# Decoder layer on one core: x and its projections ahead of the context's K sums

## The reference

```
# 1. state space part, on layernorm(x)
xp = x @ x_proj_w.T                      # 16 + 2*16 = 48 columns: dt_in, B, C
dt = softplus(dt_in @ dt_proj_w.T + dt_proj_b)
h  = exp(dt * A) * h + dt * B * x        # scan over 128 tokens, 16 states x 512 channels
y  = sum_n(h * C) + D * x;    x = x + y
# 2. cross attention, 32 heads of 128, K and V from ctx (8 x 128 x 512)
k = ctx @ w_k.T;  v = ctx @ w_v.T        # each 1024 x 4096
x = x + (hidden + attention(rmsnorm(layernorm(x)), k, v, mask, bias))
# 3. linear with low rank experts, on layernorm(x);   x = x + out
```

## Time and profile before

| | |
|---|---|
| median of three runs | 993.68 us |
| profiled execution, its time | 994.63 us |
| its span in the trace | 992.5 us |
| PE busy | 938.2 us, 95% |
| DVE busy | 645.1 us, 65% |
| ACT busy | 486.3 us, 49% |
| POOL busy | 474.4 us, 48% |
| chain that ended last | PE 61%, DVE 27%, DMA 4%, ACT 3%, issue 3%, POOL 1% |

### The profile page before, as it was taken

The page is one execution under the profiler, slowest core; times in us unless marked ns, Lnnn a source line. Parts: engine busy times, 40 slices in busy tenths (PEclk is TensorE's granted clock), DMA queues, the critical chain, the costliest instruction groups (busy, mean ns, idle before and its releaser), DMA issues.

```text
span 992.5 us, 14723 instructions
## 1 busy us (share of the span) xinstructions
PE 938.2 (95%) x4648; PEld 772.2 (78%) x4648; DVE 645.1 (65%) x819; ACT 486.3 (49%) x1058; POOL 474.4 (48%) x291
## 2 busy tenths in 40 slices
PE   8996899989898989988999999999999999999998
PEld 7665677767686767766888888888888888888867
DVE  5289889999999999752454454544545444444675
ACT  4485354546354545243455545454454554545631
POOL 2112566666666666403445444554445544455422
PEclk9977999999899999999999999999999999999999
DMA  8345655655455543215744454444444444444302
GB/s 287 112 132 159 219 169 177 196 177 180 159 185 195 170 162 133 106 47 159 265 140 142 141 149 152 135 148 137 158 143 135 144 139 151 149 135 148 104 19 85
DMA packets 92315, 149.95 MB, mean 151 GB/s; under 512 B 10192, under 2 KB 34896, under 8 KB 92160
## 3 DMA queue, kind: packets, MB, share of 16 engines
q1 hardware_dynamic: 87888, 132.72, 41.7%
q10 hardware_dynamic: 4400, 16.91, 5.5%
HBM read 113.81 MB, written 35.78 MB: 151 GB/s over the span
## 4 chain that ended last, share of the span: by engine, by line
PE 61%; DVE 27%; DMA 4%; ACT 3%; issue 3%; POOL 1%; SPq 0%; DVEq 0%; ACTq 0%; POOLq 0%
DVE misc L972 11%; PE acc L378 9%; PE acc L380 8%; PE acc L379 8%; PE misc L378 6%; PE misc L380 6%; PE misc L379 6%; PE misc L580 6%; DVE w L982 6%; DVE misc L966 6%; PE misc L606 6%; PE misc L572 3%; DMA k_scratch<-kst 2%; DMA wraw<-in_wk 1%; DMA base<-in_ctxT 1%
## 5 line engine op out<-in xcount | busy, mean ns | idle before, releaser
L1136 POOL TENSOR_TENSOR y<-y,w 128x1024 f32<-128x1024 f32 x64 | 153.5, 2398 | 144.8 <-DVE w L982 144.8
L1152 POOL TENSOR_TENSOR wq_lo<-wq_raw,wq_hi 128x512 fp32r<-128x512 f32 x64 | 83.2, 1300 | 289.4 <-ACT wq_hi L801 289.4
L1063 DVE TENSOR_TENSOR ot_lo<-misc,ot_hi 128x512 fp32r<-128x512 f32 x64 | 44.3, 692 | 172.3 <-ACT ot_hi L844 172.3
L972 DVE TENSOR_TENSOR_SCAN misc<-dA,misc 128x1024 f32<-128x1024 f32 x64 | 146.9, 2296 | 10.1 <-ACT dA L666 3.3
L837 ACT ACTIVATE prob<-prob,negm 128x128 f32<-128x128 f32 x256 | 99.8, 391 | 79.4 <-DVE negm L1047 79.4
L378 PE MATMUL acc<-wv_hi,ctx_hi 128*128 128x512 f32 x256 | 108.0, 422 | 29.9 <-ACT vst L660 17.6
L378 PE MATMUL misc<-z_hi,wq_hi 128*128 128x512 f32 x256 | 106.6, 417 | 5.4 <-POOL wq_lo L1152 5.4
L826 ACT ACTIVATE q_sb<-misc 128x512 f32<-128x512 f32 x64 | 38.2, 597 | 142.9 <-PE misc L380 142.9
L378 PE MATMUL acc<-wo_hi,ot_hi 128*128 128x512 f32 x256 | 106.8, 417 | 0.0
L379 PE MATMUL acc<-wv_lo,ctx_hi 128*128 128x512 f32 x256 | 105.5, 412 | 0.0
L380 PE MATMUL acc<-wv_hi,ctx_lo 128*128 128x512 f32 x256 | 104.5, 408 | 0.0
(11 more groups left out here) (142 smaller groups left out, 1941.2 us busy)
## 6 DMA issues: line engine op xcount, KB each, us to landing
k_scratch<-kst SPq DMA_DIRECT2D x64, 256.0 KB, 2.7
bc<-xp_scratch ACTq DMA_DIRECT2D x16, 1024.0 KB, 5.9
v_scratch<-vst SPq DMA_DIRECT2D x32, 512.0 KB, 4.0
wq_raw<-in_wq SPq DMA_DIRECT2D x64, 256.0 KB, 3.3
k_sb<-k_scratch SPq DMA_DIRECT2D x64, 256.0 KB, 2.6
v_sb<-v_scratch SPq DMA_DIRECT2D x64, 256.0 KB, 2.6
wo_raw<-in_wo SPq DMA_DIRECT2D x64, 256.0 KB, 2.9
wraw<-in_wk SPq DMA_DIRECT2D x32, 256.0 KB, 4.0
```

The lines of the kernel that those rows point to most:

```text
L972: dve.tensor_tensor_scan(h_ps, dA[c % 2][:, :, :].rearrange("p b s -> p (b s)"), h_ps, 0.0, ALU.mult, ALU.add).then_inc(da_free, 1)
L1136: pool.tensor_tensor(y[:, c], y[:, c], w[:, c], ALU.add).then_inc(y_ready, 1)
L1152: pool.tensor_tensor(wq_lo[p][:], wq_raw[p][:], wq_hi[p][:].bitcast(F32), ALU.subtract).then_inc(wq_lo_done, 1)
```

## The change

SP loads x first, then chunk 0 of K's weights and of the context, the small parameters and the mask, and then the other three chunks. DVE takes the moments of x ahead of all but the context's first low part. ACT makes chunk 0's high parts, then the inverse root for the layer norm, then the other chunks'. PE forms chunk 0 of the first four K sums, then all transposes and projections of x, then chunks 1 to 3 with `dt_proj` between them, and then K sums 4 to 7 and all eight V sums in a row. On ACT the copies of the K sums, which stood ahead of and among the steps of x, now stand behind them or among the softplus and the first exps, and all V copies stand behind `split_w(2)`.

```diff
@@ sync
-            for c in range(C):
+            def load_ctx(c):
                 sp.dma_start(wraw[:, c], a["wk"][0][:, c]).then_inc(ctx_in[c], 16)
                 sp.dma_start(ctx_raw[:, c], a["ctxT"][:, c]).then_inc(ctx_in[c], 16)
+
             for i in range(2):
                 sp.dma_start(w_tok[:, HB * i:HB * (i + 1)],
                              a["x"][HB * i:HB * (i + 1)].rearrange("b t d -> t b d")).then_inc(x_in[i], 16)
+            load_ctx(0)
             for dst, src in ((negA, "A_log"), (dskip, "D"), (dtb, "dt_b"), (xpw, "xp_w"), (dtw, "dt_w"), (lnw, "ln_w")):
                 sp.dma_start(dst[:], a[src]).then_inc(params_in, 16)
             sp.dma_start(maskraw[:], a["mask"].rearrange("b q k -> q b k")).then_inc(params_in, 16)
+            for c in range(1, C):
+                load_ctx(c)
@@ tensor
-            for c in range(C):
+            def first_sums(c):
...
-            k_sum_0(4)
-            k_sum_0(5)
+            first_sums(0)
             x_chunk(0)
             x_chunk(1)
-            k_sum_0(6)
-            x_chunk(2)
             pe.wait_ge(params_in, 16 * 7)
             x_proj(0)
+            x_chunk(2)
             x_proj(1)
             x_chunk(3)
             x_proj(2)
             x_proj(3)
-            k_sum_0(7)
-            pe.wait_ge(w_lo_done, 1)
-            v_sum(0, 0)
+            first_sums(1)
             pe.wait_ge(xp_evac, 1)
             for c in range(2):
                 dt_proj(c)
-            v_sum(0, 1)
-            for c in range(2, C):
-                dt_proj(c)
-            for b in range(2, B):
+            first_sums(2)
+            dt_proj(2)
+            first_sums(3)
+            dt_proj(3)
+            for j in range(4, KP):
+                k_sum_0(j)
+            pe.wait_ge(w_lo_done, 1)
+            for b in range(B):
                 v_sum(0, b)
@@ scalar
+            act.wait_ge(ident_done, 1)
+            act.activation(anykey[:, 0:1], ident[:, 0:1], ACT.Ln, bias=1.0)
             for c in range(C):
+                if c == 1:
+                    inverse_root(1, slice(0, B))
                 act.wait_ge(ctx_in[c], 32)
...
-            k_copy(0, 7, True)
-            split_w(2, wk_hi)
-            v_copy(0, 0, True)
...
+            softplus_exp(0)
+            softplus_exp(1)
             for n in range(2):
                 act.wait_ge(xp_stored, 16)
                 load_bc(n)
-            softplus_exp(0)
-            softplus_exp(1)
-            v_copy(0, 1, True)
             softplus_exp(2)
             softplus_exp(3)
+            k_copy(0, 0, True)
+            k_copy(0, 1, True)
             softplus_log(0)
-            v_copy(0, 2, True)
             softplus_log(1)
+            split_w(1, wv_hi)
             softplus_log(2)
             softplus_log(3)
-            v_copy(0, 3, True)
+            k_copy(0, 2, True)
+            k_copy(0, 3, True)
+            act.wait_ge(k_evac, 4)
             b_copy(0)
             act.wait_ge(a_neg, 1)
             emitted = exps(0, 2)
+            k_copy(0, 4, True)
+            k_copy(0, 5, True)
             for c in range(C):
                 act.wait_ge(u_done, c + 1)
                 act.activation(y[:, c], y[:, c], ACT.Copy, scale=dskip[:, c:c + 1]).then_inc(y0_done, 1)
-            for b in range(4, B):
+            k_copy(0, 6, True)
+            k_copy(0, 7, True)
+            split_w(2, wk_hi)
+            for b in range(B):
                 emitted = exps(emitted, due(b - B))
                 v_copy(0, b, True)
@@ vector
-            for c in range(C):
+            def low_ctx(c):
                 dve.wait_ge(ctx_hi_done, c + 1)
...
+            low_ctx(0)
             refine(1, everyone)
             for b in range(B):
                 norm(w_tok[:, b], w_tok[:, b], b).then_inc(ln1_done, 1)
+            for c in range(1, C):
+                low_ctx(c)
```

More of the change, by code:

```diff
@@ L703, in _ @@
                 act.activation(ctx_hi[:, c], ctx_raw[:, c], ACT.Copy).then_inc(ctx_hi_done, 1)
[L704 to L712, removed]
             def x_copy(c):
@@ L717, in x_copy @@
                                ACT.Copy).then_inc(xt_evac, 1)
[L719 to L723, removed]
+            for c in range(C):
+                x_copy(c)
             act.wait_ge(params_in, 16 * 7)
```

## The result

The changed kernel took 1010.23 us (median of four runs, 1008.23 to 1011.14) against 992.86 us for the kernel before (four runs, 991.8 to 995.08): 1.0163 times as long by the estimate on record, 95% interval 1.0139 to 1.0188. (The ratios in this document are these estimates; they are not quotients of the medians, here 1.0175, and differ from them by up to 0.2%.) The forecast was slower, 1002.8 us; the median lies 7.4 us above it and 0.2 us above the upper end of the range, 1010. The profiled execution took 1011.14 us, with a span of 1009.0 us, 16.5 more than before.

A forecast was written before the change was run, and what follows sets the result against it. DVE's scan bounds 126 to 409 us, but its exps tie it to PE finishing group 0's V sums. Those end 9.1 us later despite a scan start 9.2 earlier: 994.6 + 9.1 = 1003.7 profiled, 1002.8 us median; range 995 to 1010.

The forecast's parts named there:

- The tie: ACT's third exp stands ahead of group 0's last V copy; step three scans at 100.0 instead of 93.16, 6.8 later.
- Loads, norm, transposes, projections: Opening: last chunk split by 21.8, norms done at 20.5 and hidden, x's projections end at 32.0, 10.3 us earlier.
- dt projections and softplus: After x's projections: last dt projection ends at 50.5, last softplus exp at 54.5; scan starts at 72.6, 9.2 us earlier.
- The rival with the low clock: x's projections on PE start at low clock: 4.6 us more, all on the path, +13.7, 1007.4 us; chance 0.18.
- ACT to K copy 4: ACT's work from the last softplus exp: 14.1 us to 68.6, K copy 4 done at 69.2.
- The scaling of y, "costs nothing here": ACT, behind DVE's u at 72.6: four at 1.1, done at 73.8, no cost; K copy 7 done at 78.1.
- Weights: Group 1's weight load and split after K copy 7: 78.1 + 3.95 + 1.9 = 84.0, first V copy done 84.5.
- V sums: PE, group 0's V sums 2 to 7: six at 2.72, 84.6 to 100.9 against 91.83, 9.1 us later.
- Group 1: Slow K store moves along; step nine at 135.4, paced by PE, copies and stores; nothing won back, everything behind moves by 9.1.
- the likeliest case: The forecast as summed, whole kernel at 998 to 1006 us; chance 0.60.
- No hole, or group 1 before 94: Sign of a wrong forecast; right would be a DVE hole of some 16 us between scan steps two and three.
- Lateness taken back: Rival: group 1's stores land faster, both slips vanish, only step three's lateness counts: +1 to +3.5, 995 to 997; chance 0.14.

The follow-up runs named there:

- the first set: The changed kernel's first four runs against the kernel before: median 1010.23 us, ratio 1.0163; its profiled execution, the first profile, took 1011.14 us.
- the second profile: The changed kernel's same code run again, nothing changed, against the kernel before: median 1006.04 us, ratio 1.0110; profiled execution 1006.47 us.
- the reordered kernel: Changed kernel with V's split ahead of the softplus, group 1's K split behind V copy 3, ACT's copies where their sums are ready: 995.02 us, ratio 1.0014.
- the late load: Changed kernel with the second load of x (2 MB) behind group 1's K stores instead of ahead of them: 1002.63 us, ratio 1.0082.
- V's split moved: Changed kernel with the split of group 0's V weights ahead of the softplus exps instead of among the logs: 1001.76 us, ratio 1.0101.
- the long warm-up: Changed kernel with 72 warm-up transposes on PE instead of 24: 1009.67 us, ratio 1.0163.

## Why the prediction was right, and what it mis-sized

The direction and the mechanism were right: the scan started earlier and gained nothing, because the exps it needs stand on ACT behind V copies, and those behind a split that waits for late weights. The size was not: 9.1 us were forecast, 17.4 measured in the first set and 12.0 in the second. The terms that were too small are the scaling of y, put at nothing, the opening in the first profile, the wait for the weights, and, in the first profile, the slips in group 1.

*The tie.* "Step three and all later ones are tied to how far PE is with group 0's V sums" held in every kernel with `LEAD = 4`: the third exp runs ahead of V copy 7, and wherever DVE waits for it, step three scans 3.8 us ahead of group 1's first K copy (105.84 and 109.62 after, 88.11 and 91.89 reordered, 103.04 and 106.81 with the late load). In the kernel before the tie was slack at step three: the third exp was done at 90.74 and DVE came at 93.16 without a wait. From step nine's scan to the last y addition's end all of them take 282.7 us. That the early scan is worth nothing by itself is shown by the hole, and that its cause is ACT's order, not the early projections, by the reordered kernel: it keeps the order of PE and of the loads and is even with the one before.

*Loads, norm, transposes, projections.* The last chunk was split at 20.80, forecast 21.8. The norms ended at 22.52, forecast 20.5: the eight normalizations took 5.65 us instead of 3.74, beside two of POOL's low parts. This was counted as hidden and was not; then came the clock. The 48-row copy was at 35.22 (forecast 32.0), and at 32.98 in the second profile.

*dt projections and softplus.* Last softplus exp done at 58.25, forecast 54.5, second profile 54.42. So the term was right for one execution and 3.75 us short for another. The rival with the low clock put +4.6 on the projections, with the 48-row copy near 37; it lay at 35.22, so the first profile is part of that case.

*ACT to K copy 4.* 13.98 us against 14.1. Right.

*The scaling of y, "costs nothing here".* This step failed. The sum had the last of DVE's u done at 72.6; it was done at 80.5. Of these 7.9 us, 3.75 came with the opening, and 4.2 (5.45 - 1.23) from the product of the softplus that stood still behind POOL's low part of V. The scaling therefore waited 3.88 us with K copies 6 and 7 behind it, and K copy 7 was done 4.6 us late, 0.85 more than the opening's 3.75; the scan's first product took the whole 7.9. The sum took DVE's way through the softplus over from the kernel before (14.6 us), where no low part fell beside it. That such a meeting costs DVE a wait was to be seen there a little earlier: the same kind of instruction takes 0.68 us at 59.39.

```profile
51.88 4.58 POOL L1129 TENSOR_TENSOR wk_lo<-wraw,wk_hi 128x2048 fp32r<-128x2048 f32 x1 [17.51 <-ACT wk_hi L646]
...
54.42 2.60 DVE L928 TENSOR_SCALAR dA<-w 128x1024 f32<-128x1024 f32 x1 [1.46 <-ACT w L742]
```

*Weights.* 5.10 us from the last K copy's end to the split, forecast 3.95. The scaling had let K copies 6 and 7 fall together, and two stores and two loads were issued within 1.8 us (82.24 to 84.0). That is 1.15 more; that it comes from their falling together was not tested.

*V sums.* Six at 2.72 as forecast; group 1 began 5.8 us later than forecast, by 3.75 + 0.85 + 1.15 and less than 0.1 in the sums themselves.

*Group 1.* "Its slow K store moves along": it moved along and grew. The slips were 6.65 us. With steps three to nine forecast at 35.4 and measured at 36.4, this adds 1.0. That makes 135.4 + 5.84 + 1.0 = 142.24. "Nothing is won back" held. In the second profile, whose opening was on forecast, step three comes 3.35 us late and step nine only 2.2 (137.56), as group 1 took 34.2 us there instead of the 35.4 forecast: that the second set's 1006.04 lies at the edge of the likeliest case, 998 to 1006, owes 1.2 us to this.

*The rivals.* No hole, or group 1 before 94, didn't occur in the changed kernel. Lateness taken back: the slips could be removed, but by another edit (the late load), and the change itself made them larger.

*Open.* The clock in the opening, 4 us between two sets of runs. V's split was moved together with POOL's low part, so ACT's 1.9 us and DVE's stall are told apart only inside the trace. And y's scaling alone was never moved without the K copies.

## What to carry to other kernels

An engine that starts earlier gains only what its in-order suppliers deliver: before moving a stage forward, find the third or fourth instruction of it on the supplying engine, and what stands ahead of that one. When a block of copies is moved behind another job, price each copy by the sum, store and reload that wait for it, not by its own 0.6 us. And running further ahead is not free either: an instruction that waits for its consumer's buffer stops all that is written behind it.

## What the runs showed of the hardware

A DVE product with two SBUF operands that began inside a POOL operation took 5.45 us instead of 1.23, in every profile with V's split among the logs, and 1.23 in every one with it moved. Small ones suffer alike: DVE's 8-column product at 15.57 took 1.27 us beside POOL's low part (15.53, 1.29), and the same kind at 14.96 and 15.16, ahead of it, 0.17.

A 256 KB store takes 2.6 us in the median over the kernel, and 9.83 when it is issued 2.4 us behind a 2 MB load on the same queue (108.03 and 110.39). With the load moved, the first six K copies of group 1 waited for no store (106.81 to 120.41).

Transposes held the clock up here. Behind 72 of them in 11.00 us, with 0.68 us of idle time after, four K matmuls took 1.19 us at a granted clock of 1.00 (2.4 GHz); behind 24 in 5.23 us and 6.02 us of idle time they took 2.07 at 0.50. (The last 48 took about 0.12 us each and the first ones 0.22, but the granted clock is 1.00 in both stretches, so it doesn't account for that.) The Trainium skill, "TensorE: Matmul & The Clock Gate", Part 4, says that the full rate doesn't engage for transposes; these rows speak against it. Matmuls over 16 rows are less clear: eight `dt_proj` matmuls at full pace (3.69) were followed by 2.03 us for four K matmuls in the second profile, but by 1.20 with V's split moved and with the long warm-up.
